# Attention and experts, twice over: idle identity products in five places and a new order of calls

## What is computed

```python
x = x + L0_xattn(layernorm(x), ctx, bias=fside, mask)     # scores + bias, softmax, values, Wo
x = x + L0_ffn(layernorm(x), w_router, wi, wo)            # top 2 of 8, capacity 64, gelu
x = x + L1_xattn(layernorm(x), ctx, fside + fside + fside_SxS2)
x = x + L1_ffn(layernorm(x), gate_w, gate_b, expert_w, expert_b)   # top 2 of 10, 2 of them null
```

## Time and profile before

| | |
|---|---|
| median of 3 runs | 374.14 us (373.89 to 374.92) |
| profiled execution | 372.75 us, span 371.0 us |
| TensorE matmul busy | 318.2 us, 86% |
| VectorE busy | 261.1 us, 70% |
| GpSimd busy | 183.1 us, 49% |
| ScalarE busy | 173.2 us, 47% |
| mean granted TensorE clock | 0.937 of full |

### The profile page before, as it was taken

How to read it: one execution, slowest core, us unless ns; L and a number is a source line. 1 busy time by engine, 2 the same in 40 slices (tenths; PEclk the granted TensorE clock), 3 DMA queues, 4 the chain that set the end, 5 groups by cost and what they waited for, 6 DMA issues and landing times.

```text
span 371.0 us, 8972 instructions
## 1 busy us (share of the span) xinstructions
PE 318.2 (86%) x3628; PEld 237.4 (64%) x3633; DVE 261.1 (70%) x639; ACT 173.2 (47%) x321; POOL 183.1 (49%) x197
## 2 busy tenths in 40 slices
PE   3789767899999999999999999999787987798771
PEld 2468465577888778778788778885444653556420
DVE  4669665977596396852679566667779689986762
ACT  3144313375844827349285464735341363346331
POOL 7356283785708357163364714155362266624515
PEclk9999977999999999999999999999976699689995
DMA  7994970050504000000000000000000000000000
GB/s 191 256 374 107 333 213 2 2 145 3 138 10 113 27 2 2 3 2 2 2 3 2 2 2 2 3 0 2 3 0 31 0 3 0 30 2 3 0 28 28
DMA packets 26427, 19.15 MB, mean 52 GB/s; under 512 B 1973, under 2 KB 24339, under 8 KB 26387
## 3 DMA queue, kind: packets, MB, share of 16 engines
q1 hardware_dynamic: 26387, 18.59, 17.3%
HBM read 17.53 MB, written 1.05 MB: 50 GB/s over the span
## 4 chain that ended last, share of the span: by engine, by line
PE 50%; DVE 25%; issue 10%; ACT 7%; POOL 6%; DMA 1%; POOLq 0%; DVEq 0%; ACTq 0%
PE PB L1046 9%; DVE SC L1640 6%; PE HBK L1135 6%; PE SP L1027 5%; PE SP L1008 4%; PE EBK L1150 4%; POOL SC L408 4%; DVE mx L1642 3%; ACT PT L632 3%; DVE acc L1847 3%; DVE rc L1647 3%; PE HBK L1210 2%; PE SP L1012 2%; PE HBK L1158 2%; PE EBK L1210 2%
## 5 line engine op out<-in xcount | busy, mean ns | idle before, releaser
L408 POOL TENSOR_TENSOR SC<-SC,mx 128x1232 f32<-128x1232 f32 x32 | 74.0, 2313 | 98.9 <-DVE mx L1642 98.8
L632 ACT COPY PT<-SP 128x512 f32<-128x512 f32 (+1 forms) x96 | 44.5, 526 | 44.5 <-PE SP L1027 38.4
L624 ACT ACTIVATE SC<-SC 128x1232 f32<-128x1232 f32 x32 | 39.4, 1234 | 26.8 <-POOL SC L408 26.7
L1027 PE MATMUL SP<-ident,SC 128*128 128x128 f32 x320 | 47.2, 292 | 4.6 <-ACT SC L624 4.0
L1642 DVE TENSOR_REDUCE mx<-SC 128x16 f32<-128x1232 f32 x32 | 46.0, 1436 | 1.1
L1027 PEld LDWEIGHTS SP<-ident,SC 128*128 128x128 f32 x320 | 39.1, 151 | 10.8 <-ACT SC L624 6.2
L1647 DVE RECIPROCAL rc<-PB 128x128 f32<-128x128 f32 x32 | 30.5, 954 | 21.0 <-PE PB L1046 20.7
L1135 PE MATMUL HBK<-ein,wi_s 128*128 128x128 f32 x256 | 36.1, 284 | 2.1 <-ACT hT L653 2.1
L1135 PEld LDWEIGHTS HBK<-ein,wi_s 128*128 128x128 f32 x256 | 31.1, 191 | 7.5 <-ACT hT L653 4.9
L1008 PE MATMUL SP<-KB,qT 32*128 32x308 f32 x256 | 28.8, 512 | 8.1 <-DVE SC L1640 4.3
L1046 PE MATMUL PB<-PT,VB 128*32 128x128 f32 x768 | 30.1, 294 | 5.7 <-ACT PT L632 4.9
(11 more groups left out here) (188 smaller groups left out, 569.7 us busy)
## 6 DMA issues: line engine op xcount, KB each, us to landing
BI<-in_fside_Bx16xSxS SPq DMA_DIRECT2D x8, 1232.0 KB, 6.6
wi_s<-in_L_ffn_wi SPq DMA_DIRECT2D x1, 2048.0 KB, 8.9
X<-in_x SPq DMA_DIRECT2D x4, 256.0 KB, 4.3
out<-acc SPq DMA_DIRECT2D x3, 256.0 KB, 2.2
MI<-in_mask_BxSxS_ik SPq DMA_DIRECT2D x8, 77.0 KB, 5.0
ew_s<-in_L_ffn_expert_w SPq DMA_DIRECT2D x1, 512.0 KB, 4.1
out<-acc SPq DMA_DIRECT2D x2, 128.0 KB, 1.7
ctxn<-in_ctx SPq DMA_DIRECT2D x1, 154.0 KB
```

The lines of the kernel that those rows point to most:

```text
L408: g.tensor_tensor(S4, S4, m4, ALU.subtract).then_inc(s["shifted"], 1)
L624: sc.activation(S3, S3, ACT.Exp).then_inc(s["probs"], 1)
L632: sc.copy(PT[:, c0:c1, :].rearrange("p c t -> p (c t)"), SP[:, n, 0:(c1 - c0) * P]).then_inc(s["PTs"], 1)
L1027: last = te.transpose(SP[:, n, (c - c0) * P:(c - c0 + 1) * P], SC[i % 2][:, c * P:(c + 1) * P], ident[:])
```

## The change

A new call `warm(a, i)` on TensorE waits until `resid` is at t and then does three products of the identity with itself into the unused quarter of PB. Nothing reads them. It is called in five places: ahead of `weigh_values` of the tiles (0,2), (0,3), (5,2) and (7,1), and ahead of `attn_scores` (6,0). Besides, calls are moved by one to five places, some further, in the lists of TensorE, VectorE, ScalarE and GpSimd; no call is added or taken away otherwise, and the waits inside the calls stay. SyncE's list is unchanged. The core of the diff, by engine:

```diff
 # GpSimd
             block_rows()
+            head_rows()
+            a_rstd(0)
+            block_keys(0, 0, "k_kb")
             identity_bf16()
-            a_rstd(0)
-            head_rows()
             mask_out(0, 0)
-            block_keys(0, 0, "k_kb")
...
 # ScalarE
             copy_PT(0, 0, 1)
+            copy_keys(1)
             softmax_exp(0, 1)
-            copy_keys(1)
...
+            softmax_exp(0, 2)
             copy_gate()
-            softmax_exp(0, 2)
+            copy_PT(0, 2, 0)
             a_xTcopy(1)
-            copy_PT(0, 2, 0)
...
 # TensorE
+            def warm(a, i):
+                pe.wait_ge(s["resid"], NT * a + i)
+                for _ in range(3):
+                    te.matmul(PB[:, 3 * P:4 * P], ident[:], ident[:], start=True, stop=True)
...
             attn_scores(0, 2, 0)
-            values(1)
             weigh_values(0, 0)
             value_bias(1)
             turn(0, 1, 0)
+            values(1)
             turn(0, 1, 1)
             project(0, 0, 0)
             attn_scores(0, 3, 0)
+            values(2)
             turn_gate()
             weigh_values(0, 1)
-            a_xTr(1)
-            values(2)
             turn(0, 2, 0)
             turn(0, 2, 1)
+            a_xTr(1)
+            project(0, 1, 0)
             query(1, 0)
-            project(0, 1, 0)
+            warm(0, 2)
             weigh_values(0, 2)
             turn(0, 3, 0)
             turn(0, 3, 1)
+            attn_scores(1, 0, 0)
             project(0, 2, 0)
-            attn_scores(1, 0, 0)
             attn_scores(1, 1, 0)
+            warm(0, 3)
             weigh_values(0, 3)
             project(0, 3, 0)
             values(3)
             f_xTr(0)
             turn(1, 0, 0)
+            logits0(0)
             turn(1, 0, 1)
-            logits0(0)
...
             experts(4, 0)
+            project(5, 1, 1)
+            turn(5, 2, 0)
             a_xTr(6)
-            turn(5, 2, 0)
-            project(5, 1, 1)
             turn(5, 2, 1)
+            warm(5, 2)
             weigh_values(5, 2)
...
             experts(4, 2)
+            warm(6, 0)
             attn_scores(6, 0, 1)
             f_xTr(5)
             experts(4, 3)
...
             experts(5, 3)
+            f_xTr(6)
             attn_scores(7, 1, 1)
-            f_xTr(6)
...
             attn_scores(7, 3, 1)
+            warm(7, 1)
             weigh_values(7, 1)
+            turn(7, 2, 0)
             experts(6, 0)
-            turn(7, 2, 0)
             turn(7, 2, 1)
...
 # VectorE
             softmax_max(0, 2, 0)
+            add_bias(1)
+            invert(0, 0)
+            normalise(0, 0)
             a_stats(1, 0)
-            invert(0, 0)
-            add_bias(1)
-            normalise(0, 0)
             mask_values(1)
...
             normalise(0, 2)
-            mask_values(2)
+            softmax_max(1, 0, 0)
             add_residual(0, 2, 0)
-            softmax_max(1, 0, 0)
             softmax_max(1, 1, 0)
             invert(0, 3)
```

More of the change, by code:

```diff
@@ L482, in _ @@
             f_rstd(0)
+            triangles()
             split_x(0)
@@ L490, in _ @@
             combine_weights(0, 2)
+            block_keys(1, 1, "k_kb1")
             combine_weights(0, 3)
             mask_out(2, 0)
-            block_keys(1, 1, "k_kb1")
+            a_rstd(3)
             block_keys(3, 0, "k_kb")
+            shift(2, 0)
+            f_rstd(1)
+            residual_bias(2, 0)
             mask_out(2, 1)
[L496 to L499, removed]
+            shift(2, 1)
+            shift(2, 2)
             split_x(1)
-            shift(2, 1)
             combine_weights(1, 0)
-            shift(2, 2)
+            shift(2, 3)
             combine_weights(1, 1)
-            mask_out(3, 0)
-            shift(2, 3)
             combine_weights(1, 2)
             combine_weights(1, 3)
+            mask_out(3, 0)
             a_rstd(4)
+            f_rstd(2)
             residual_bias(3, 0)
-            f_rstd(2)
-            mask_attn(4)
             shift(3, 0)
@@ L531, in _ @@
             residual_bias(4, 1)
+            a_rstd(5)
             shift(4, 3)
-            a_rstd(5)
+            mask_attn(5)
             combine_weights(3, 2)
-            mask_attn(5)
+            block_keys(3, 1, "k_kb1")
             combine_weights(3, 3)
@@ L704, in _ @@
             copy_PT(1, 0, 1)
+            softmax_exp(1, 1)
             copy_PT(1, 1, 0)
@@ L726, in _ @@
             f_xTcopy(1)
+            copy_eo(0, 0)
             gelu(0, 5)
-            copy_eo(0, 0)
+            route_exp("m_route", ROUTE0, 2, "m_exp", NE, 1)
             copy_PT(2, 0, 0)
-            route_exp("m_route", ROUTE0, 2, "m_exp", NE, 1)
             copy_PT(2, 0, 1)
+            copy_eo(0, 1)
             softmax_exp(2, 1)
             gelu(0, 6)
-            copy_eo(0, 1)
             copy_eo(0, 2)
+            copy_PT(2, 1, 0)
             gelu(0, 7)
-            copy_PT(2, 1, 0)
+            a_xTcopy(3)
             copy_PT(2, 1, 1)
+            softmax_exp(2, 2)
             copy_eo(0, 3)
-            softmax_exp(2, 2)
             copy_PT(2, 2, 0)
-            a_xTcopy(3)
             copy_ein(1, 0)
-            copy_PT(2, 2, 1)
             softmax_exp(2, 3)
             copy_ein(1, 1)
+            copy_PT(2, 2, 1)
             copy_CT(1, 0)
@@ L763, in _ @@
             route_exp("m_route", ROUTE0, 2, "m_exp", NE, 2)
+            copy_PT(3, 0, 0)
+            copy_eo(1, 2)
+            copy_PT(3, 0, 1)
             softmax_exp(3, 1)
-            copy_PT(3, 0, 0)
-            copy_PT(3, 0, 1)
-            copy_eo(1, 2)
             gelu(1, 6)
             gelu(1, 7)
+            a_xTcopy(4)
             copy_eo(1, 3)
@@ L807, in _ @@
             copy_PT(4, 2, 0)
+            copy_ein(3, 0)
+            softmax_exp(4, 3)
             copy_PT(4, 2, 1)
-            copy_ein(3, 0)
             copy_ein(3, 1)
-            softmax_exp(4, 3)
+            copy_CT(3, 0)
             a_xTcopy(5)
-            copy_CT(3, 0)
             copy_CT(3, 1)
+            copy_CT(3, 2)
+            copy_CT(3, 3)
             copy_PT(4, 3, 0)
-            copy_CT(3, 2)
             copy_PT(4, 3, 1)
-            copy_CT(3, 3)
             gelu(3, 0)
@@ L822, in _ @@
             gelu(3, 3)
+            gelu(3, 4)
             copy_eo(3, 0)
-            gelu(3, 4)
             f_xTcopy(4)
@@ L1292, in _ @@
             logits0(1)
+            down(0, 1)
             turn(2, 0, 0)
+            turn(2, 0, 1)
             up(0, 6)
-            turn(2, 0, 1)
-            down(0, 1)
             weigh_values(2, 0)
@@ L1300, in _ @@
             up(0, 7)
+            a_xTr(3)
             turn(2, 1, 0)
@@ L1374, in _ @@
             up(2, 2)
+            down(2, 0)
+            up(2, 3)
             project(3, 3, 0)
-            up(2, 3)
-            down(2, 0)
+            attn_scores(4, 1, 1)
             up(2, 4)
-            attn_scores(4, 1, 1)
             up(2, 5)
@@ L1400, in _ @@
             weigh_values(4, 1)
-            turn(4, 2, 1)
             dispatch(3, 0)
             dispatch(3, 1)
+            turn(4, 2, 1)
+            project(4, 1, 1)
             turn_C(3, 0)
-            project(4, 1, 1)
+            turn(4, 3, 0)
             a_xTr(5)
             turn_C(3, 1)
+            turn_C(3, 2)
             weigh_values(4, 2)
-            turn(4, 3, 0)
-            turn_C(3, 2)
+            turn_C(3, 3)
             turn(4, 3, 1)
-            turn_C(3, 3)
             query(5, 1)
+            up(3, 0)
             project(4, 2, 1)
-            up(3, 0)
             attn_scores(5, 0, 1)
@@ L1941, in _ @@
             without_first(1)
+            invert(2, 0)
             best(1, 1)
@@ L1957, in _ @@
             normalise(2, 1)
+            a_stats(4, 1)
             add_residual(2, 1, 0)
@@ L1984, in _ @@
             best(2, 1)
+            a_norm(4, 1)
             is_best(2, 1)
+            invert(3, 0)
             ranked(2, 1)
-            invert(3, 0)
             first_best(2, 1)
@@ L2118, in _ @@
             logit_max(5)
+            weigh_expert(4, 3, 0)
             logit_less(5)
-            weigh_expert(4, 3, 0)
+            weigh_expert(4, 3, 1)
             exp_sum(5)
@@ L2181, in _ @@
             logit_max(6)
+            weigh_expert(5, 3, 0)
+            weigh_expert(5, 3, 1)
             logit_less(6)
+            weigh_expert(5, 3, 2)
             exp_sum(6)
-            weigh_expert(5, 3, 0)
             exp_inverse(6)
+            weigh_expert(5, 3, 3)
             gate_probs(6)
-            weigh_expert(5, 3, 1)
             best(6, 0)
-            weigh_expert(5, 3, 2)
             is_best(6, 0)
-            weigh_expert(5, 3, 3)
             ranked(6, 0)
@@ L2202, in _ @@
             kept(6)
+            invert(7, 0)
             kept_sum(6)
```

136 lines of the change are left out of this document (64 added, 72 removed).

## The result

The changed kernel takes 377.48 us (median of 16 executions, 375.31 to 378.61), the kernel before 373.88 (16 executions, 370.75 to 376.21). The ratio is 1.0092, with a 95% interval of 1.0066 to 1.0118: it is slower by 0.9%, where 1.0% faster was forecast. The profiled execution took 377.31 us.

What follows compares the result with a forecast made beforehand. TensorE was taken as the bound from 68 to 250 us, taking turns with VectorE after. 372.75 + 0.65 - 2.3 - 1.7 - 0.5 = 368.9, as a median 370.3 us; range 366.5 to 376.5.

Steps and rivals of the forecast that it cites:

- The order: Some 120 moved calls on four engines: 0.5 us gained, between 2 gained and 2 lost; nothing booked in the head.
- a new fall: Rival: moved calls leave a new thin stretch, up to 3.2 us lost at half clock; median 377.5 us, chance 0.21.
- The idle products: Five calls at 0.65 us each, 1.3 at half clock, mostly covered by waits; sum booked 0.65 us lost.
- The cover at (0,3) and (6,0): Idle products there hide behind slack, 1.5 us at (0,3), later VectorE reader at (6,0); nothing booked.
- The fall at 50.8: Head: the call (0,3) keeps the clock up; 1.8 us gained there, head in all 2.3, between 0 and 2.9.
- clock 1.00 from 49 to 57: Sign that the forecast holds: TensorE at full clock from 49 to 57 us, with value products at 1.1.
- two signs of being wrong: Weighing (0,3) later than 47.6 us and the projection behind it later than 51.2.
- The fall at 269: The call (6,0) keeps the clock up; experts take 1.92 instead of 3.58 us; 1.7 gained, between 0 and 1.7.
- The middle: From 68 to 250 us TensorE idles 6.3 us, the most any order could get; the order's 0.5 gained was booked.
- The range: Low end 366.5 us, with both falls and more gone; high end 376.5, within the new fall's case.
- neither goes: Rival: both falls stay, since the moment of a clock change differs between runs; median 375.1 us, chance 0.19.

Runs made afterwards that it cites:

- e1: Changed kernel with the first calls of before on GpSimd and TensorE (head undone): 373.89 us, ratio 1.0004 to the kernel before.
- e5: Kernel before with only its first calls on GpSimd and TensorE ordered as in the change: 375.99 us, ratio 1.0059.
- e10: Kernel before with only TensorE's keys(0) put ahead of a_xTr(0): 376.69 us, ratio 1.0063.
- e9: Kernel before with only GpSimd's first five calls in the order of the change: 374.70 us, ratio 1.0014.
- e7: Changed kernel plus six idle products ahead of the first transposes and one behind the first transposed weights: 375.33 us, ratio 1.0014 to the kernel before.
- e8: Kernel before plus six idle products ahead of the first transposes and three behind the first transposed weights: 371.80 us, ratio 0.9958.
- e2: Changed kernel with VectorE's weigh_expert(6,3,3) back ahead of gate_logits(7) (tail undone): 375.55 us, ratio 1.0030 to the kernel before.
- e3: Changed kernel without the five warm calls of idle products: 379.99 us, ratio 1.0070 to the kernel before.
- e12: Changed kernel with head and moved expert sum undone and without the five warm calls: 375.76 us, ratio 1.0037 to the kernel before.
- e4: Changed kernel with both the head and the moved expert sum undone: 373.13 us, ratio 0.9996 to the kernel before.

## Why the prediction was wrong

*The step that failed is "The order": "In the head ... VectorE sets the pace with the maxima and the normalised a_xn, so I book nothing."* I looked at values(1) only, near 24 us. The two moves in the first 8 us were before me, and the diff shown ahead of the prediction even leaves out TensorE's swap. There the chain is one thread from X to the first scores, without slack: GpSimd's a_rstd(0) behind five small operations (0.53 us), keys(0) ahead of the transposes (0.4 us alone), together 0.47 at the query product. These could be read off the trace before. Beyond them stood the clock's first rise, which the page hides: 1.5 of the 1.99 us at the first maximum are products at half clock. The head costs 3.6 us by the medians (e1), 1.8 to 2.2 on the old kernel (e5), where most of it comes with TensorE's order (e10: 2.5; GpSimd's, e9: 0.6, not told from none). The direct part is half a microsecond; that the rest is the clock is read from the traces, and e7 and e8 bear it out.

*The same step, tail.* One call of VectorE moved by two places: 1.9 us by the medians (e2), where nothing was booked. The waiter was experts(7,0), whose first wait is for that very sum. The wait of 0.78 us is covered (0.03 us in e3); what costs is the fall of the clock at 355, 1.7 us. That is the rival "a new fall", again at a place not named.

*The idle products: size off by a third.* The term was 0.65 a call:

```profile
40.51 0.94 PE L1055 MATMUL PB<-ident 128*128 128x128 f32 x6
41.38 0.86 PE L1046 MATMUL PB<-PT,VB 128*32 128x128 f32 x24
...
50.43 1.35 PE L1055 MATMUL PB<-ident 128*128 128x128 f32 x6
...
56.28 1.28 PE L944 MATMUL EBK<-WT,shared 128*128 128x64 f32 x10
```

The values follow 0.87 us after the call's start, not 0.65, and a call that meets the low clock takes 1.35. That makes 0.2 us more at each exposed place. The cover at (0,3) and (6,0) held, as booked.

*The fall at 50.8: right in kind, paid for elsewhere.* The lateness drops from 3.96 us at the row maximum (1,1) to 2.07 at (1,2): 1.9 gained, where 1.8 was forecast for the fall itself. But another fall came at 48.0 and hit the scores (1,1):

```profile
48.08 1.41 PE SP L1008 x8
49.49 1.15 PE SP L1012 x4
```

These two lines are 1.1 us longer than at full clock, all on the chain. It is the rival "a new fall", at a place that I hadn't named. The sign "clock 1.00 from 49 to 57" failed with it, and two signs of being wrong came: the weighing (0,3) starts at 51.71 us and the projection behind it at 54.89, not by 47.6 and 51.2. In the trace of e1, with another head, the clock holds from 15 to 63 us and the lateness goes from 1.59 to -0.30; in that of e3, without the calls, it goes from 1.98 to 2.34. So in these traces the call (0,3) does hold the clock, as forecast.

*The fall at 269: right in size, and by luck.* The lateness goes from 3.70 at the row maximum (6,0) to 2.04 at (6,1): 1.66, the number forecast. But the call (6,0) is not shown to be the cause: without it the same 1.66 are gained (e3), as they are in e8, e9 and e12. And the new order had lost 1.2 us just before (2.73 at (5,2), 3.91 at (5,3); likewise in e1 to e4 and e12), of which I booked nothing.

*The middle.* 0.5 gained was booked; the lateness is 2.34 at the reciprocal (1,2) and 2.42 at (4,1): nothing.

*The range.* The rival of a new fall had the right sign with 377.5 and 0.21 of the chance; the range ended at 376.5, inside that case. Of the mechanism it named one part, the falls at 48 and 355 (1.1 and 1.7 us); the head it did not have, so that its number came close is partly luck. The rival "neither goes" said that the places of the low stretches vary between executions; that is so (table above), and it was the better reading of the spread from 370.75 to 376.21.

What stays open: which part of e4's missing 1.2 us (4.35 instead of 5.5) is the clock's draw, whether TensorE's order delays the first rise, and what the idle products are worth (2.5 and 2.6 us by the medians in the new order, nothing in the old). The two groups of e4's times suggest the first, but only one execution of each kernel has a trace.

## What to carry to other kernels

When hundreds of calls move and a few are added, go through the ends of the kernel first, where the chain is a single thread: an operation put ahead of a link there can cost up to its whole length, and it moves the products against the clock. Read TensorE's speed from the durations of equal products, not from the clock's row alone, above all before the first change that it records. And a single profile is one draw of the clock: the term "a low stretch sits here" needs several executions, or an interval as wide as the stretch.

## What was unexpected of the hardware

The first rise of the clock lies anywhere from 9.9 to 20.8 us without early work, and the same head gave 9.9 in one kernel's trace and 19.6 in another's. With nine idle products of 128 columns in the first 7 us, where TensorE mostly waits, it came at 5.1 to 7.8 (seven of them: 5.4), and the old kernel had a ratio of 0.9958, where the searched order had 1.0092. The clock can be lost again within seven microseconds of that (5.4 to 12.2 in e7). And the profile's mean granted clock did not follow the time: 0.950 in the changed kernel's trace against 0.937 before, because the stretch before the first rise counts as full. With that stretch taken at half, which is an estimate from the two first rises, both would be 0.92.
